# Adds of neighbouring pairs of one expert without a wait between them, in a kernel of attention and a mixture of experts

## The reference

```python
x = x + attn(layernorm(x), Wq, Wk, Wv)          # causal, softmax(q k' / 16) v
xf = layernorm(x)                                # [4096, 256]
shared = (silu(xf @ shared_gate') * (xf @ shared_up')) @ shared_down'
probs = sigmoid(xf @ router_w' + routing_bias)   # [4096, 8]
scores, idx = top_k(probs, 2); scores = scores / sum(scores)
w = zeros(4096, 8) with scores at idx
g, u = silu(einsum('th,ehi->tei', xf, gate_w)), einsum('th,ehi->tei', xf, up_w)
x = x + shared + einsum('tei,eih,te->th', g * u, down_w, w)
```

## Time and profile before

| what | us |
|---|---|
| median of 3 runs | 575.85 (572.58 to 577.54) |
| the profiled execution | 575.28 |
| its span, first to last instruction | 573.2 |
| TensorE busy | 521.4 (91% of the span) |
| VectorE, ScalarE, GpSimd busy | 364.7, 301.2, 288.5 |
| mean granted TensorE clock | 0.977 |

### The profile page before, as it was taken

How to read it: one execution, slowest core, us unless ns; L and a number is a source line. 1 busy time by engine, 2 the same in 40 slices (tenths; PEclk the granted TensorE clock), 3 DMA queues, 4 the chain that set the end, 5 groups by cost and what they waited for, 6 DMA issues and landing times. The chain is left out here.

```text
span 573.2 us, 14884 instructions
## 1 busy us (share of the span) xinstructions
PE 521.4 (91%) x4757; PEld 426.7 (74%) x4757; DVE 364.7 (64%) x962; ACT 301.2 (53%) x580; POOL 288.5 (50%) x241
## 2 busy tenths in 40 slices
PE   4879898999999997977899999999999999999980
PEld 3557686777878785865677788788788888888870
DVE  5768986987898884976466555544554454445540
ACT  3989697776787574642243434333343343344440
POOL 4557768676676665565204334444335344444353
PEclk9999899999999998999999999999999999999995
DMA  8789749879595935342536864754846545446633
GB/s 266 209 158 218 167 111 193 189 161 217 136 210 136 198 83 142 115 139 90 155 69 86 103 103 69 101 66 68 96 65 92 84 69 77 56 59 77 76 38 37
DMA packets 139350, 68.54 MB, mean 120 GB/s; under 512 B 114608, under 2 KB 132336, under 8 KB 139280
## 3 DMA queue, kind: packets, MB, share of 16 engines
q1 hardware_dynamic: 126128, 48.84, 42.0%
q0 software_dynamic: 13152, 18.76, 19.1%
HBM read 19.46 MB, written 23.08 MB: 74 GB/s over the span
## 5 line engine op out<-in xcount | busy, mean ns | idle before, releaser
L2168 PE MATMUL bank<-xn2t,w 128*128 128x256 f16 x1608 | 186.7, 274 | 4.2 <-DVE th L1634 2.1
L2168 PEld LDWEIGHTS bank<-xn2t,w 128*128 (+1 forms) x1608 | 155.8, 98 | 28.4 <-issue 4.4
L1625 DVE SCALAR_TENSOR_TENSOR th<-th,bank 128x512 f32<-128x512 f32 x83 | 56.7, 683 | 64.0 <-ACT th L970 60.4
L2192 PE MATMUL bank<-w,h 128*128 (+1 forms) x768 | 91.6, 272 | 0.2 <-DVE h L1451 0.2
L970 ACT ACTIVATE th<-bank 128x512 f32<-128x512 f32 x83 | 49.2, 592 | 74.4 <-PE bank L2168 47.3
L924 ACT ACTIVATE h<-th 128x512 f16<-128x512 f32 (+1 forms) x69 | 42.9, 622 | 83.5 <-DVE th L1634 78.4
L2192 PEld LDWEIGHTS bank<-w,h 128*128 128x128 f16 x768 | 73.8, 98 | 10.5 <-issue 1.3
L847 POOL DMA_INDIRECT out<-p,wm x28 | 44.3, 1582 | 71.0 <-ACT p L1304 21.2
L720 POOL TENSOR_TENSOR w<-wst,w 128x768 f16<-128x768 f32 x36 | 59.4, 1652 | 33.0 <-ACT w L924 32.4
L1451 DVE TENSOR_TENSOR h<-th,h 128x512 f16<-128x512 f32 (+1 forms) x69 | 47.1, 683 | 39.7 <-ACT h L924 36.6
L744 POOL DMA_INDIRECT rows<-xrow,sidx x56 | 56.4, 1008 | 15.7 <-issue 13.6
(11 more groups left out here) (193 smaller groups left out, 807.3 us busy)
## 6 DMA issues: line engine op xcount, KB each, us to landing
wst<-w_all SPq DMA_DIRECT2D x36, 384.0 KB
x<-x SPq DMA_DIRECT2D x8, 512.0 KB, 5.6
out<-x SPq DMA_DIRECT2D x8, 512.0 KB
rows<-xrow POOLq DMA_DIRECT2D x1, 1192.5 KB, 6.6
rows<-xrow,sidx POOLq DMA_INDIRECT x56
out<-p,wm POOLq DMA_INDIRECT x28, 3.9
xn2t<-rows SPq DMA_TRANSPOSE x26
wm<-rows SPq DMA_DIRECT2D x26, 9.0 KB
```

What stands on the lines that cost most here:

```text
L1625: d.scalar_tensor_tensor(out=tb, in0=tb, scalar=1.0, in1=G[half][:, :], op0=ALU.add, op1=ALU.mult).then_inc(f_sg, 1)
L2168: ins = mm(dst, w_ap(j, ws, m * MAT + k * I + (2 * half + i) * P, P), moving(ms * KD + k), start=(cnt == 0), stop=(cnt == 3 * KD - 1))
L2192: ins = mm(o[:, a * D:(a + 1) * D], hb[:, (hs * KI + i) * TT + a * P:(hs * KI + i) * TT + (a + 1) * P], w_ap(j, ws, 2 * MAT + i * D, D), s ...
```

## The change

- Of the 26 pairs, 18 are now taken in blocks of 512 rows of one expert: `QUADS` = 9 blocks, each of which gives two pairs. `place(n)` maps the pair to its place in the tables: pairs 0 to 15 are blocks 0 to 7, pairs 24 and 25 are block 8, and pairs 16 to 23 are `MORE` = 8 pieces of 256 rows as before.
- `partners(n)`: n is even, pairs n and n + 1 are halves of one block, and their adds stand next to each other in the order. Then `before` of the second is that of the first, so it doesn't wait for the first's adds (their tokens are different ones), and `after` of the first is that of the second. This holds for n = 2, 4, ... 14 and 24.
- In `FIRST_ADDS` and on GpSimd, pair 2 moves behind single 4, next to pair 3.
- Tables: `table_of_quads` has 9 entries and 20 steps (the pairs' had 26 and 19), `table_of_singles` 28 steps for 20, `table_of_halves` 17 as before, and a new `table_of_pairs` of 8 entries and 9 steps stands behind `ffn(SHARED + 2, 0)`. `tab3` is full only after it.
- The last down products: chunks 0 and 1 for both halves of the rows, then chunks 2 and 3 for the first half, then for the second.

```diff
+QUADS = (TOPK * T // HP - 7 * E) // 8
+MORE = PAIRS - 2 * QUADS
+EARLY = 2 * (QUADS - 1)
-FIRST_ADDS = (("pair", 0), ("single", 0), ("single", 1), ("pair", 1), ("single", 2), ("single", 3), ("pair", 2),
-              ("single", 4))
+FIRST_ADDS = (("pair", 0), ("single", 0), ("single", 1), ("pair", 1), ("single", 2), ("single", 3), ("single", 4),
+              ("pair", 2))
+def partners(n):
+
+    return n % 2 == 0 and (n < EARLY or n == PAIRS - 2) and ADDED["pair", n + 1] == ADDED["pair", n] + 32
+
+def place(n):
+
+    return n + 2 if EARLY <= n < PAIRS - 2 else n - MORE if PAIRS - 2 <= n < PAIRS else n
+
 def after(kind, n):
 
-    return ADDED.get((kind, n), 0)
+    return ADDED.get((kind, n + 1 if kind == "pair" and n >= 0 and partners(n) else n), 0)
 
 def before(kind, n):
 
+    if kind == "pair" and n and partners(n - 1):
+        return before(kind, n - 1)
     return ADDED[kind, n] - (32 if kind == "pair" else 16)
...
-        T_STEPS, T2_STEPS, T3_STEPS = 19, 20, 17
+        T_STEPS, T2_STEPS, T3_STEPS = 20, 28, 26
...
-                return sp.value_load(start_tab[0:1, ds(n, 1)], min_val=0, max_val=ROWS - TT)
+                return sp.value_load(start_tab[0:1, ds(place(n), 1)], min_val=0, max_val=ROWS - TT)
...
-            const(cc.iota(tneg[:, 0:PAIRS], pattern=[[-TT, PAIRS]], base=0, channel_multiplier=0, **imp))
+            const(cc.iota(tneg[:, 0:2 * QUADS], pattern=[[-TT, 2 * QUADS]], base=0, channel_multiplier=0, **imp))
+            const(cc.iota(tneg[:, 2 * QUADS:PAIRS], pattern=[[-TT, MORE]], base=0, channel_multiplier=0, **imp))
...
                 y_add_single(3)
+                y_add_single(4)
                 y_add(2)
-                y_add_single(4)
...
+            def table_of_pairs():
+
+                c = Chain(dve, tab3, T3_STEPS, 0, T3_STEPS - 9)
+                c.last()
+                table(c, MORE, 1, 2 * QUADS, TT, INC_P, PREV_P, BASE_P)
+                assert c.k == c.per, c.k
...
-            table_of_pairs()
+            table_of_quads()
...
             ffn(SHARED + 2, 0)
+            table_of_pairs()
             single_h(3)
...
-                for n, chunks in enumerate(pieces):
-                    pe.wait_ge(f_lo, t * 2 + n + 1)
-                    for a in range(2):
+                for low, chunks, parts in pieces:
+                    pe.wait_ge(f_lo, t * 2 + low)
+                    for a in parts:
                         for i in chunks:
...
-                down_parts(t, j0, ((0, 1), (2, 3)))
+                down_parts(t, j0, ((1, (0, 1), (0, 1)), (2, (2, 3), (0, 1))))
                 last_gate_up(t + 1, j1, pair_moving(1))
-                down_parts(t + 1, j1, ((0, 1), (2,), (3,)))
+                down_parts(t + 1, j1, ((1, (0, 1), (0, 1)), (2, (2,), (0,)), (3, (3,), (0,)), (3, (2, 3), (1,))))
```

More of the change, by code:

```diff
@@ L1726, in _, with sums_before, table @@
             r_ = lambda i: tf[0:1, i * E:(i + 1) * E]
-            CF, LEFT, TWOS, INC, PREV, VAL, TMP, ONE, STEP, BASE, USED, ODD = (r_(i) for i in range(12))
+            (EIGHTS, FOURS, TWOS, LEFT, INC, PREV, VAL, TMP, ONE, STEP, BASE, USED, ODD,
+             INC_P, PREV_P, BASE_P) = (r_(i) for i in range(16))
             CNT = PT2[0:1, 0:E]
-            def table(c, n, first, unit):
+            def sums_before(c, counts, inc, prev):
+                c.then(d.tensor_tensor_scan(inc, ONE, counts, 0.0, ALU.mult, ALU.add)); c.last()
+                c.then(d.tensor_tensor(prev, inc, counts, ALU.subtract))
+            def table(c, n, sets, first, unit, inc, prev, rows_of):
                 t3 = lambda t_: t_[0:1, 0:n * E].rearrange("p (t e) -> p t e", e=E)
@@ L1734, in table @@
                 t1 = lambda i: tsum[0:1, i * PAIRS:i * PAIRS + n]
[L1735 to L1740, removed]
+                per_set = lambda t_: t_.unsqueeze(2).to_broadcast([1, n, sets])
+                of_sets = lambda t_, at_: t_[0:1, at_:at_ + n * sets].rearrange("p (t s) -> p t s", s=sets)
+                c.then(d.tensor_tensor(t3(oh), t3(tio), per_piece(inc), ALU.is_ge)); c.last()
+                c.then(d.scalar_tensor_tensor(out=VAL, in0=prev, scalar=float(unit), in1=rows_of, op0=ALU.mult,
                                               op1=ALU.add))
@@ L1744, in table, with used, less_used, table_of_quads @@
                 c.then(d.tensor_tensor(STEP[:, 0:E - 1], VAL[:, 1:E], VAL[:, 0:E - 1], ALU.subtract))
-                c.then(d.tensor_scalar(w_tab[0:1, first:first + n], t1(1), 1.0, float(E), ALU.add, ALU.min)); c.last()
+                c.then(d.tensor_scalar(of_sets(w_tab, first), per_set(t1(1)), 1.0, float(E), ALU.add, ALU.min)); c.last()
                 c.then(d.tensor_tensor(t3(ot), t3(oh), per_piece(STEP), ALU.mult)); c.last()
                 c.then(d.tensor_reduce(t1(0), t3(ot), X, ALU.add)); c.last()
[L1748 to L1753, removed]
+                c.then(d.scalar_tensor_tensor(out=of_sets(tsum, PAIRS), in0=per_set(t1(0)), scalar=VAL[:, 0:1],
+                                              in1=of_sets(tneg, first), op0=ALU.add, op1=ALU.add)); c.last()
+                c.then(d.tensor_scalar(of_sets(start_tab, first), of_sets(tsum, PAIRS), float(SPARE), None, ALU.min))
+            def used(c, prev, n, counts):
+                c.then(d.tensor_scalar(USED, prev, -1.0, float(n), ALU.mult, ALU.add)); c.last()
+                c.then(d.scalar_tensor_tensor(out=USED, in0=USED, scalar=0.0, in1=counts, op0=ALU.max,
+                                              op1=ALU.min)); c.last()
+            def less_used(c, o, i, k):
+                c.then(d.scalar_tensor_tensor(out=o, in0=USED, scalar=float(-k), in1=i, op0=ALU.mult, op1=ALU.add))
+            def table_of_quads():
                 c = Chain(dve, tab, T_STEPS, 0)
@@ L1759, in table_of_pairs @@
                 dve.wait_ge(cnt_mm, 1)
[L1761 to L1763 removed]
+                c.then(d.tensor_scalar(ti[0:1, 4 * E:5 * E], CNT, float(HP - 1), None, ALU.add)); c.last()
+                for k, unit in enumerate((2 * TT, TT, P, HP)):
+                    c.then(d.tensor_single_scalar(ti[0:1, k * E:(k + 1) * E], ti[0:1, 4 * E:5 * E],
                                                   unit.bit_length() - 1, ALU.logical_shift_right))
                 c.last()
[L1766 removed]
+                c.then(d.tensor_copy(tf[0:1, 0:4 * E], ti[0:1, 0:4 * E]))
                 c.then(d.scalar_tensor_tensor(out=BASE, in0=CNT, scalar=-float(TT), in1=base[0:1, 0:E],
                                               op0=ALU.add, op1=ALU.add)); c.last()
[L1770 removed]
+                sums_before(c, EIGHTS, INC, PREV)
+                table(c, QUADS, 2, 0, 2 * TT, INC, PREV, BASE)
+                assert c.k == c.per, c.k
             def table_of_singles():
@@ L1774, in table_of_singles @@
                 dve.wait_ge(tab, T_STEPS)
-                c.then(d.scalar_tensor_tensor(out=ODD, in0=TWOS, scalar=-2.0, in1=LEFT, op0=ALU.mult, op1=ALU.add))
-                c.then(d.tensor_scalar(USED, PREV, -1.0, float(PAIRS), ALU.mult, ALU.add)); c.last()
+                c.then(d.scalar_tensor_tensor(out=ODD, in0=TWOS, scalar=-2.0, in1=LEFT, op0=ALU.mult, op1=ALU.add)); c.last()
                 c.then(d.tensor_reduce(TMP[:, 0:1], ODD, X, ALU.add))
-                c.then(d.scalar_tensor_tensor(out=USED, in0=USED, scalar=0.0, in1=CF, op0=ALU.max,
-                                              op1=ALU.min)); c.last()
+                used(c, PREV, QUADS, EIGHTS)
                 c.then(d.scalar_tensor_tensor(out=TWOS[:, E - 1:E], in0=TMP[:, 0:1], scalar=float(HALVES) + 0.5,
                                               in1=TWOS[:, E - 1:E], op0=ALU.is_ge, op1=ALU.add))
[L1783 to L1788, removed]
+                less_used(c, FOURS, FOURS, 2)
+                less_used(c, LEFT, LEFT, 8)
+                less_used(c, BASE_P, BASE, 2 * TT); c.last()
+                less_used(c, TWOS, TWOS, 4)
+                sums_before(c, FOURS, INC_P, PREV_P); c.last()
+                used(c, PREV_P, MORE, FOURS)
+                less_used(c, TWOS, TWOS, 2)
+                less_used(c, LEFT, LEFT, 4)
+                less_used(c, BASE, BASE_P, TT); c.last()
+                c.then(d.tensor_scalar(BASE, BASE, float(TT - P), None, ALU.add))
+                sums_before(c, TWOS, INC, PREV)
+                table(c, SINGLES, 1, PAIRS, P, INC, PREV, BASE)
+                assert c.k == c.per, c.k
             def table_of_halves():
@@ L1792, in table_of_halves @@
                 dve.wait_ge(tab2, T2_STEPS)
[L1794 to L1800, removed]
-                c.then(d.tensor_scalar(BASE, BASE, float(P - HP), None, ALU.add)); c.last()
-                table(c, HALVES, PAIRS + SINGLES, HP)
+                used(c, PREV, SINGLES, TWOS)
+                less_used(c, LEFT, LEFT, 2)
+                less_used(c, BASE, BASE, P); c.last()
+                c.then(d.tensor_scalar(LEFT, LEFT, 0.0, None, ALU.max))
+                c.then(d.tensor_scalar(BASE, BASE, float(P - HP), None, ALU.add)); c.last()
```

(7 more changed lines are left out.)

10 lines of the change are left out of this document (5 added, 5 removed).

## The result

The changed kernel took 571.64 us in the median of 14 runs, beside 577.27 us for the kernel before in 14: a ratio of 0.9917, interval 0.9893 to 0.9941 (the two medians alone give 0.9902). So the change is worth between half and nearly one per cent. The forecast was a gain of 5.4 us (0.94%, on the border of 1%) and a time of 570.4 us, in a range of 566.8 to 574.5. The measured gain is 4.8 us by the first ratio and 2.7 to 3.0 us by the three later ones.

What follows compares the result with a forecast made beforehand. GpSimd's backlog of ordered adds was taken to bound the end. The profiled 575.28 us less 5.4, with tables and longer waits at nothing, gave 569.9; the median lies 0.57 higher, so 570.4, range 566.8 to 574.5.

Steps and rivals of the forecast that it cites:

- What bounds the kernel: At the end: GpSimd's adds, 5.1 and 5.5 us behind their data, set the end, not TensorE's products.
- Partners in the tail: Pairs 24 and 25: the wait of 2.92 us becomes 0.30, 2.62 us off the end if nothing else changed.
- Pair 15: Last early partner: starts between 476.2 and 478.1 us instead of 480.81, 4.6 to 2.7 us earlier; 4.6 taken.
- The 76.8 us behind it stay as they are.: From pair 15 to pair 24: 12 landings without partners take 76.8 us as before, so pair 24 comes at 553.0.
- the prediction's own sign of being wrong: Pairs 16 to 23: their lag stays at 7 us, or the products of the first groups come later.
- The end that follows: Pair 25's adds at 558.55 and 560.42 instead of 565.84, with 0.2 handover: gain 5.4 us, bounds 4.6 and 5.6.
- The tables: VectorE's table work: longer singles' table and new pairs' table cost nothing; uncovered, 1.3 and 0.7 us.
- The longer waits: ScalarE's copies and SyncE's loads, where after now includes the partner's adds: nothing, in both directions.
- rival D: SyncE's queue meets the longer wait, next tile's rows come late in every group: 8.6 us slower, 584.5; 5%.
- A: Only the tail's wait goes, as landings between pairs 15 and 24 stretch: 2.62 us won, 573.2; 12%.
- C: Start of the routed half, 264 to 270 us: hole grows or shrinks by 2.1 us, 568.3 or 572.5; 7% each side.
- B: The end is set by something with its own pace, for example the DRAIN: no change, 575.9; 8%.

Runs made afterwards that it cites:

- the three later ones: The unaltered changed kernel compared again with the kernel before, three times: ratios 0.9950, 0.9954 and 0.9949.
- e4: Against the kernel before, only the new tables; no partners, order of adds and of last products as before: ratio 1.0002.
- e0: The changed kernel run again with nothing altered: median 572.67 us, ratio to the kernel before 0.9950.
- e1: The changed kernel with partners(n) only for n = 24, tables and orders as in the change: ratio to the kernel before 0.9938.
- e2: The changed kernel with partners(n) for n = 2, 4, ... 14 but not 24: ratio to the kernel before 0.9941.
- e11: As late blocks, but pair 25 waits for pair 24's landing again: last add 5.32 us behind the start of the last 12 down products.
- e7: The changed kernel with small plain loads replacing the transposing row loads of pairs 15 to 25: wait for pair 15's landing 3.01 us.
- late blocks: Against the changed kernel, blocks of 512 are pairs 0, 1 and 10 to 25, pieces of 256 pairs 2 to 9: ratios to before 0.9887, 0.9867.

## Why the prediction was right, and where it was not

*What bounds the kernel.* Right: the end hung on GpSimd's adds, and the two removals of waits move it, from 10.08 without partners to 8.42 with the last one and 4.7 with both where the lag is gone. The tables change nothing that can be measured (e4: 1.0002). The total times don't tell the parts apart: e0, e1 and e2 have 0.9950, 0.9938 and 0.9941 on one chip.

*Partners in the tail.* The wait fell to 0.30 where there was a lag (e0, e1). Without a lag the wait of 3.08 is worth 0.6 us (e11). Both as the prediction's steps put it, since it didn't add the 2.62 to the rest.

*Pair 15.* Forecast at 476.2, found at 475.90, in part by luck: the forecast let it start 0.33 us behind its data, and it starts 0.99 behind them, but the data came 0.96 earlier in this execution. In every profile of a kernel in which pairs 14 and 15 are partners it adds with no lag.

*"The 76.8 us behind it stay as they are."* This is the step that failed. It measured 76.1 in the first profile, 82.0, 77.9 and 76.1 in the others. The 76.1 are TensorE's own pace, since at both ends the adds waited for their data. The prediction had 1.7 us to spare at pair 24 (free at 556.4, needed at 558.1 or so) and gave the term no spread. What it missed has two parts. First, lag is not only carried from pair 15 on but made again behind it: between the copies of pairs 15 and 16 lie 11 us (474.09 to 485.06), and in them three sets of adds with three landings, which took 14.9 us before and 15.8, 18.3, 16.5 and 16.5 in the changed kernel. Second, what is won at pair 15 is in part paid back there. An add on time lands beside SyncE's row load, and the lag grows by 4.8 to 7.3 us up to pair 16; it grows by 4.0 before and in e1, where pair 15 is late (4.9 in e4), and by 4.0 in e7 without that load. From there TensorE's 7.86 us per pair stand against 3.44 of issuing plus a landing: with 3.1 us it catches up 1.3 per pair, with 4.7 it loses. Whether the lag is gone by pair 24 depends on where a few landings fall. It was gone in two of four profiles, 1.8 us and without effect on the end in a third, and 5.9 in e0. There the prediction's own sign of being wrong came true: the lag of pairs 16 to 23 stayed at 5.2 to 8.1.

*The end that follows.* 5.4 us were forecast, 4.74 found. The handover is the term: I took 0.2 between nothing and 1.01, and it is 0.78. The other 0.1 is the product order: the copy's end was to come 2.02 us behind the start of the last products, and came 2.11 behind it, as before (2.12). That the first time, 571.64, lies near 570.4 is luck in part, since the three later ratios are worth only 2.7 to 3.0 us.

*The tables.* VectorE's idleness 2.30 us where 2.5 was forecast, no cost (e4). The wait for single 3's transpose was anything from 0.2 to 2.7 over all profiles.

*The longer waits.* No profile has a row of TensorE that waits for rows of a pair; rival D had nothing for it.

*The rivals.* A (only the tail's wait, 2.62) describes e0 nearly: 8.47 instead of 4.8, though for another reason than a stretch of all 12 landings: the twelve waits from pair 15 to pair 24 sum to 45.5 us there and 40.6 before, and two of them (4.98 for 3.00 behind pair 15, 6.05 for 4.74 before pair 22) make two thirds of the difference. It had 12%, and one of four profiles had it. C's shift ahead of pair 0 exists and is larger than forecast, 6 us, but between executions of one kernel (277.7 to 283.7 in the changed one, 279.2 to 285.3 in late blocks) and not through the change. B and D are out.

The mean of the four distances is 5.67, 3.84 us less than 9.51, which is 0.67%; the four ratios' mean is 0.9943. They agree within the ratios' intervals, though the 9.51 is one profile's. Why the stretch from pair 0 to the last products took 275.2 to 277.2 us in the changed kernel and 274.9 before isn't settled: e4 without partners had 277.3, e1 with one 274.2.

## What to carry to other kernels

Where an ordered chain of small transfers runs behind the engine that feeds it, look for where its lag is made, not only where it ends: a wait removed before that point can be given back there in part, and one removed behind it stays won. Ask too what a transfer that now comes on time will run beside. Put the few allowed overlaps where the feeding is fastest and work per transfer smallest, here in the pairs behind the last single. And give a chain of a dozen landings the spread of landings, not the sum of one profile.

## What the hardware showed that I had not expected

In the last group a GpSimd indirect DMA started 0.7 to 0.8 us after what it waited for, whether a copy or a landing: 0.78 behind the copy at pair 24 (551.21 to 551.99), 0.74 behind the landing in e11 (553.49 + 3.90 = 557.39 to 558.13). In the groups before it was 0.99 behind a copy. The chain of waits of the changed kernel, around pair 24:

```profile
546.87 3.86 DMA out<-phl,wm
...
550.75 0.46 ACT p L1422
...
551.28 0.71 issue
551.99 1.56 POOL out L861
553.56 0.30 issue
553.86 3.81 DMA out<-p,wm
557.67 0.28 issue
```

Of the 3.0 us between two ordered adds, 2.2 to 2.3 are the landing behind the 1.57 of issuing, and the rest is this start. In the earlier trace rows the two stand together as 2.92 of "issue". The Trainium skill ("DMA: Bandwidth & Descriptors", Anatomy of one DMA — SWDGE (gpsimd) path) gives about 2.0 us fixed; the trace's 3.8 to 3.9 from issue to landing contain 1.57 of issuing, and with that taken off 2.2 to 2.3 are left, near the page's figure.
